# Sub-experts: half of the gates read from DRAM as repeated rows, and one product of four on GpSimd

## The chip, the cores and the metric

The kernel runs as one program on one core of a Trainium2 chip. The metric is device microseconds of one execution, lower is better. Before the change it takes 2109.84 us (median of three runs, 2108.4 to 2111.88).

## What is computed

The model is a chain of eight layers on 16 samples of 102 tokens with 192 features each. The change touches the sixth layer, a bank of small experts. Cut to what matters, with n over the 1632 tokens, s over 8 sets, m over 64 sub-experts of a set, r over 16 features, h over 32 hidden units:

```
z = einsum('nd,sdr->nsr', xf, P)
scores = einsum('nsr,smr->nsm', z, C)
topv, topi = top_k(scores, 4)
w = softmax(topv)
h = gelu(einsum('nsr,nskrh->nskh', z, W1[topi]) + b1[topi])
yl = einsum('nskh,nskhr->nskr', h, W2[topi]) + b2[topi]
comb = einsum('nskr,nsk->nsr', yl, w)
out = gelu(comb @ G1 + g1b) @ G2 + g2b
```

The kernel gathers nothing: it computes the hidden values of all 512 sub-experts for all tokens and multiplies each by its gate, which is zero for a sub-expert that was not chosen.

## The kernel before, in words

Two functions matter. `fusion_and_gates` (tiles named `l2b_...`) ends layer 5 and makes z and the gates. Per sample it transposes the gates of all 512 sub-experts into one PSUM bank as `[128, 4, 102]` (row = 64 * odd + m, four blocks r), copies them to `gT` in f32, and splits them into three bf16 parts whose sum is the f32 value: part 0 by a ScalarE copy (L1447), the rest by a VectorE subtraction (L1606), part 1 by another ScalarE copy (L1456), part 2 by GpSimd (L1159). SyncE stores the parts to the DRAM tensor `g_parts` after every four samples.

`sub_experts` (tiles `l2s_...`) is the stage of this case. Its work is 256 pairs, in the hand-written list `order`: (half of the samples, r, odd, t, pair). A pair is 128 hidden units (4 sub-experts of 32) for 8 samples, done as two chunks of 408 columns. For each pair:

- TensorE makes the hidden sums, two bf16 products of 128 x 408 (`up_products`, L2277).
- ScalarE applies bias and gelu to both chunks at once, 128 x 816 (L2352), into `hidden`.
- TensorE spreads the gates: the 4 gates of a chunk, each as three bf16 rows, are multiplied with a 0/1 matrix of 96 x 128, so that each gate stands on 32 partitions of a PSUM bank (`gates_spread`, L2285). Two per pair.
- VectorE multiplies hidden by gates, one chunk of 128 x 408 f32 at a time (L2382), into the ring `gated`.
- TensorE multiplies `gated` with the f32 down weights, four chunks at a time in four column groups (`second`, L2297); the sums of 32 such calls gather in one PSUM bank, and VectorE then adds them to `comb` (L2367, L2369).

Two pairs (four chunks) are called a group below; there are 128 groups. TensorE's order is written out in a loop: `up_products(p + 1)`, two spreads, and after every second pair a `second` of the group before. The gate banks are three, the `hidden` buffers three, the `gated` ring has ten chunks. All transfers of the stage are issued by SyncE (six by ScalarE) at its start, in program order, without a wait: z parts, up weights, gate parts, down weights for k = 0 to 3, then z and gate parts of the second half, then `pack_l3a` for the next layer. After the 128 groups comes a short tail: hidden products and results of four quarters.

Two transfers elsewhere in the program are used below for comparison. Layer 4 stores the tensor `up_pairs` (L772) in eight transfers of 512 KB; each goes from 128 partitions, written to DRAM as 8 sets x 16 rows x 2048 bf16 values. Layer 8 stores `xln` (L2488, L2489) from 102 partitions, written as 102 tokens x 16 samples x 192 (or 64) values.

Of the kernel before, what the change touches and what calls it, by code (L numbers as in the profile page):

```python
# [1023 lines left out]
def fusion_and_gates(nc, g, dram):  # L1024
# [8 lines left out]
    with ExitStack() as stack:  # L1033
# [13 lines left out]
        g_left = spare["l0a"].take(128, 4, L)  # L1047
# [14 lines left out]
        gT = m.sb("gT", [128, 4, GB, L])  # L1062
        g_parts = m.sb("g_parts", [128, 2, 3, 4, GB, L], BF16)
# [45 lines left out]
        gT_view = gT_bank.rearrange("p (r n) -> p r n", r=4)  # L1109

# [9 lines left out]
        def _(sp):  # L1120
            for c in range(G):
# [41 lines left out]
        def _(pe):  # L1163
# [91 lines left out]
            def bias_products(c, half):  # L1255
# [4 lines left out]
                for r in range(2):  # L1260
                    row = 64 * (c % 2) + HP * r
                    last = pe.matmul(gT_bank[row:row + HP], wf.at("b2", RG)[:, 2 * half + r, :], gT[:, 2 * half + r, :, :],
                                     start=True, stop=True)
# [91 lines left out]
        def _(act):  # L1355
# [49 lines left out]
            def step(t):  # L1405
# [37 lines left out]
                if 0 <= n < B:  # L1443
                    act.wait_ge(gT_ps, n + 1)
                    if n >= 2 * GB and n % GB == 0:
                        act.wait_ge(g_stored[n // GB % 2], 48 * (n // GB // 2))
# [34 lines left out]
        def _(dve):  # L1481
# [89 lines left out]
            def step(t):  # L1571
# [29 lines left out]
                if 0 <= e < B:  # L1601
# [4 lines left out]
                    dve.tensor_tensor(g_left[:, :, :], gT_view, g_parts[:, e // GB % 2, 0, :, e % GB, :], ALU.subtract)\  # L1606
# [566 lines left out]
def sub_experts(nc, g, dram):  # L2173
# [9 lines left out]
    pairs, per_sum_bank = len(order), len(order) // 2  # L2183
    with ExitStack() as stack:  # L2184
# [4 lines left out]
        gs = [[m.sb(f"gs{half}{k}", [96, 2, 2, HALF, L], BF16) for k in range(4)] for half in range(2)]  # L2189
# [7 lines left out]
        hid_ready, gated_ready = m.sem("hid_ready"), m.sem("gated_ready")  # L2197
# [12 lines left out]
        def gate_bank(n):  # L2210
            return ps[:, 1, n % gates, 0:NG]
# [9 lines left out]
        def gate_parts(eng, half, k):  # L2221
            for a in range(3):
                for n in range(2):
                    rows = 64 * (k % 2) + 32 * n
                    eng.dma_start(gs[half][k][32 * a:32 * (a + 1), n, :, :, :],
                                  g["g_parts"][a, rows:rows + 32, 2 * (k // 2):2 * (k // 2) + 2,
                                               half * HALF:(half + 1) * HALF, :]).then_inc(parts_loaded[half][k], 16)

        @block.sync
        def _(sp):  # L2230
# [17 lines left out]

            sp.dma_start(spread_raw, dram["sub_spread"]).then_inc(spread_loaded, 16)
            for half in range(2):  # L2250
                for k in range(4):
                    parts(half, k)
                    if not half:
                        up_weights(k)
                    if half or k:
                        gate_parts(sp, half, k)
                    if not half:
                        down_weights(k)
                    if not half and k == 2:
                        sp.dma_start(comb[:, :, :, :, :], g["sub_bias"]).then_inc(sums_loaded, 16)  # L2260
                        sp.dma_start(per_sum[:, :, :, :, :], g["sub_per_sum"]).then_inc(sums_loaded, 16)
# [4 lines left out]
        def _(pe):  # L2266
# [14 lines left out]
            def gates_spread(n):  # L2281
                half, r, odd, t, pair = order[n // 2]
                if n >= gates:
                    pe.wait_ge(gated_ready, n - gates + 1)
                pe.matmul(gate_bank(n), spread[:, t % 8, :], gs[half][2 * r + odd][:, t // 8, pair, chunk(n % 2), :],  # L2285
                          start=True, stop=True).then_inc(gate_ps, 1)

            def second(n):
                if n % per_sum_bank == 0 and n:
                    pe.wait_ge(comb_ready, n // per_sum_bank)  # L2290
                pe.wait_ge(gated_ready, n + group)
                for at in range(n, n + group):
                    half, r, odd, t, pair = order[at // 2]
                    if not half and t == 0 and pair == 0 and at % 2 == 0:
                        pe.wait_ge(down_loaded[2 * r + odd], 16)
                    row = HP * (2 * (at % 2) + pair)
                    last = pe.matmul(sums[row:row + HP, :], down[2 * r + odd][:, pair, t, :], gated[:, at % ring, :],  # L2297
                                     start=(odd == 0 and t == 0), stop=(odd == 1 and t == MT - 1))
                if (n + group) % per_sum_bank == 0:
# [748 lines left out]
```

## Time and profile before

| what | value |
|---|---|
| median of three runs | 2109.84 us |
| span of the profiled execution | 2092.6 us |
| what lies around the span, taken as the rest of the median | 17.2 us |
| `sub_experts`: first up product to last `second` | 1308.7 to 1631.5 us |
| busy over the whole span: PE, DVE, ACT, POOL | 1823.8, 1217.6, 837.4, 379.2 us |

The profile gives no run time of its own for the profiled execution beside its span; the runs shown agree within 0.2%. Times of rows are microseconds from the span's start. PE is TensorE's matmul, PEld its weight load, DVE VectorE, ACT ScalarE, POOL GpSimd, SPq SyncE issuing transfers. PEclk is the granted clock of TensorE (1.00 is 2.4 GHz, 0.50 is 1.2 GHz), DMA share the mean busy share of the core's 16 DMA engines, GB/s what they moved.

### The profile page before, as it was taken

How to read it: one execution, taken by the hardware profiler on the slowest of the kernel's cores; microseconds unless marked ns; L12 is line 12 of the kernel's file. 1: busy time of each engine (PE TensorE's matmuls, PEld its weight loads, DVE VectorE, ACT ScalarE, POOL GpSimd, SP SyncE). 2: the span in 40 equal slices, each digit the busy share in tenths (PEclk: the TensorE clock that was granted, in tenths of full speed). 3: DMA queues.
4: the chain of work that ended last, by engine and by line, in shares of the span. 5: the costliest groups of instructions: out<-in, count | busy, mean ns of one | idle time of the engine just before them, and what ended most of it. 6: DMA issues, size and time to landing. Idle time of an engine off the chain costs nothing. (4 is left out here: it accounts for less than half of the span.)

```text
span 2092.6 us, 38743 instructions
## 1 busy us (share of the span) xinstructions
PE 1823.8 (87%) x13908; PEld 1324.8 (63%) x14000; DVE 1217.6 (58%) x3641; ACT 837.4 (40%) x1667; POOL 379.2 (18%) x380
## 2 busy tenths in 40 slices
PE   4989969987886799888898875999999999979997
PEld 3678759966674699677665542333333688647886
DVE  1478842237998322378635554788888567891221
ACT  1145413324552111145435554677667355311111
POOL 1100112133312232331001111000000000223543
PEclk8999969998996899889999877999999999999999
DMA  5000245520003455102000115900000000304663
GB/s 202 1 1 0 108 131 178 187 74 18 14 0 141 142 186 182 38 19 87 0 1 17 38 49 145 292 2 1 1 1 1 24 1 0 134 22 124 197 173 65
DMA packets 83838, 156.75 MB, mean 75 GB/s; under 512 B 22389, under 2 KB 57941, under 8 KB 82805
## 3 DMA queue, kind: packets, MB, share of 16 engines
q1 hardware_dynamic: 63669, 134.71, 19.7%
q0 software_dynamic: 19552, 19.63, 3.9%
q8 instruction: 80, 1.31, 0.3%
q10 hardware_dynamic: 480, 0.63, 0.1%
q14 instruction: 57, 0.47, 0.1%
HBM read 125.04 MB, written 29.48 MB: 74 GB/s over the span
## 5 line engine op out<-in xcount | busy, mean ns | idle before, releaser
L2382 DVE TENSOR_TENSOR l2s_gated<-l2s_hidden,ps 128x408 f32<-128x408 f32 x512 | 262.8, 574 | 58.3 <-PE ps L2285 58.0
L2352 ACT ACTIVATE l2s_hidden<-ps,pack_l2f 128x816 f32<-128x816 f32 x256 | 227.2, 938 | 98.1 <-PE ps L2277 97.4
L129 PE MATMUL ps<-pack_const 128*128 128x512 bf16 x496 | 149.7, 437 | 42.2 <-PEq L163 15.3
L2285 PE MATMUL ps<-l2s_gs,l2s_spread 96*128 96x408 bf16 x512 | 150.8, 341 | 0.3 <-DVE l2s_gated L2382 0.3
L2277 PE MATMUL ps<-l2s_zs,l2s_up 128*128 128x408 bf16 x512 | 133.0, 342 | 14.5 <-DMA l2s_gs<-g_parts 14.5
L1895 PE MATMUL ps<-l_down,l_hidden 128*128 x792 | 139.8, 326 | 0.0
L1895 PEld LDWEIGHTS ps<-l_down,l_hidden 128*128 128x128 f32 x792 | 127.3, 190 | 0.4
L129 PEld LDWEIGHTS ps<-pack_const 128*128 128x128 bf16 x588 | 59.7, 109 | 102.1 <-issue 64.6
L2297 PE MATMUL ps<-l2s_gated,l2s_down 128*32 128x408 f32 x1024 | 114.3, 518 | 4.0 <-DVE l2s_comb L2369 3.7
L2277 PEld LDWEIGHTS ps<-l2s_zs,l2s_up 128*128 128x128 bf16 x512 | 39.8, 97 | 119.5 <-ACT l2s_hidden L2352 82.2
L1854 POOL DMA_INDIRECT l_xt<-rows_in,l_tokens x66 | 63.1, 956 | 255.7 <-PE ps L1867 196.5
L1878 PE MATMUL ps<-l_xtT,l_up 128*128 128x128 f32 x792 | 101.2, 278 | 3.4 <-DVE l_xtT L2145 3.4
L1878 PEld LDWEIGHTS ps<-l_xtT,l_up 128*128 128x128 f32 x792 | 98.3, 194 | 4.4 <-DVE l_xtT L2145 4.4
L2285 PEld LDWEIGHTS ps<-l2s_gs,l2s_spread 96*128 96x128 bf16 x512 | 50.1, 98 | 79.1 <-DVE l2s_gated L2382 49.5
L1974 ACT ACTIVATE l_hidden<-ps,l_down 128x128 f32<-128x128 f32 x198 | 54.8, 375 | 89.9 <-PE ps L1883 89.9
L2823 DVE TENSOR_TENSOR l3c_expert_hidden<-l3c_expert_gate,ps 128x204 f32<-128x204 f32 x96 | 30.9, 364 | 98.0 <-ACT l3c_expert_gate L2651 98.0
L1977 ACT ACTIVATE l_hidden<-ps 128x384 f32<-128x384 f32 x66 | 28.8, 488 | 143.2 <-PE ps L1883 143.2
L2651 ACT ACTIVATE l3c_expert_gate<-ps 128x204 f32<-128x204 f32 x96 | 27.4, 338 | 145.1 <-PE ps L2587 145.1
L2694 POOL DMA_INDIRECT out<-l3c_part,l3c_chosen_place x32 | 57.4, 1793 | 98.9 <-DVE l3c_part L2813 90.3
L2145 DVE TENSOR_SCALAR l_xtT<-ps,pack_l1r 128x128 f32<-128x128 f32 x66 | 24.0, 406 | 81.2 <-PE ps L1867 81.2
L2145 DVE TENSOR_SCALAR l_xtT<-ps,pack_l0r 128x128 f32<-128x128 f32 x66 | 24.1, 407 | 78.1 <-PE ps L1867 78.1
L496 POOL MEMSET l3a_v<- 102x408 f32 x2 | 1.0, 518 | 358.6 <-POOLq L2184 358.6
(468 smaller groups left out, 3985.0 us busy)
## 6 DMA issues: line engine op xcount, KB each, us to landing
l_up<-in_l_up SPq DMA_DIRECT2D x66, 576.0 KB, 3.8
l3c_wg<-in_l_gate SPq DMA_DIRECT2D x16, 576.0 KB, 4.9
l3c_wu<-in_l_up SPq DMA_DIRECT2D x16, 576.0 KB, 6.2
l3c_wd<-in_l_down SPq DMA_DIRECT2D x16, 576.0 KB, 3.9
slots_out<-l_y SPq DMA_DIRECT2D x66, 96.0 KB, 2.3
l_down<-in_l_down SPq DMA_DIRECT2D x8, 675.0 KB, 9.2
g_parts<-l2b_g_parts SPq DMA_DIRECT2D x12, 408.0 KB, 4.4
l_down<-in_l_down SPq DMA_DIRECT2D x8, 576.0 KB, 7.3
```

Source lines behind the costliest of these rows:

```text
L129: pe.matmul(bank, halves[:, 0:128], halves[:, :], start=True, stop=True)
L1854: pool.indirect_dma_start(xt[:, i % 3, :], None, xs, bass.IndirectOffsetOnAxis(ap=tokens[:, i:i + 1], axis=0))\
L1878: pe.matmul(hid_bank(i, half)[:, t * 128:(t + 1) * 128], up[:, i % 3, n * 128:(n + 1) * 128], xtT[:, i % 2, 0, :], start=(t == 0), stop=Fa ...
L1895: last = pe.matmul(y_bank(i), hidden[:, i % 2, t, :], wd[:, t * D:(t + 1) * D], start=(t == 0), stop=(t == FM - 1))
L1974: last = act.activation(hidden[:, i % 2, n, :], hid_bank(i, half)[:, t * 128:(t + 1) * 128], func, bias=b1[:, n:n + 1])
L2145: last = dve.tensor_scalar(xtT[:, i % 2, c, :], turned(i)[:, c * 128:(c + 1) * 128], w.at("wide_g")[:, c:c + 1], w.at("wide_b")[:, c:c + 1 ...
L2277: last = pe.matmul(ps[:, 0, 2 * (p % 2) + c, 0:NG], up_parts[k][:, pair, t * 128:(t + 1) * 128], zs[half][k][:, pair, chunk(c), :], start= ...
L2285: pe.matmul(gate_bank(n), spread[:, t % 8, :], gs[half][2 * r + odd][:, t // 8, pair, chunk(n % 2), :], start=True, stop=True).then_inc(ga ...
L2297: last = pe.matmul(sums[row:row + HP, :], down[2 * r + odd][:, pair, t, :], gated[:, at % ring, :], start=(odd == 0 and t == 0), stop=(odd ...
L2352: act.activation(hidden[:, p % kept, :, :], ps[:, 0, 2 * (p % 2):2 * (p % 2) + 2, 0:NG], ACT.Gelu_apprx_tanh, bias=w.at("b1")[:, s * MT + ...
L2382: dve.tensor_tensor(gated[:, n % ring, :], hidden[:, n // 2 % kept, n % 2, :], gate_bank(n), ALU.mult)\
L2694: pool.indirect_dma_start(table, bass.IndirectOffsetOnAxis(ap=chosen_place[:, a, e:e + 1], axis=0), part[:, e % 2, a, :], None, compute_op ...
```

## The change

Half of the gates, those of the pairs with pair = 1, are no longer spread by TensorE. `fusion_and_gates` keeps the bf16 parts of blocks 0 and 2 only, and stores blocks 1 and 3 in f32 to a new DRAM tensor `g_whole`. `sub_experts` reads them back with one transfer per group: four rows of 816 values (3264 bytes), each repeated 32 times, into one of six buffers `whole` of 128 x 816. The first six are issued between the up weights and the down weights of k = 0, the others behind all transfers of the first half, each waiting until its buffer is free. Of a group's four chunks VectorE multiplies two with gates in PSUM (L2417) and one with gates in `whole` (L2424), and GpSimd the fourth with gates in `whole` (L2395). `hidden` gets four buffers, `gated` shrinks to eight chunks, and `second` now comes after the next up products.

```diff
-        g_left = spare["l0a"].take(128, 4, L)
+        g_left = spare["l0a"].take(128, 2, L)
...
-        gT = m.sb("gT", [128, 4, GB, L])
-        g_parts = m.sb("g_parts", [128, 2, 3, 4, GB, L], BF16)
+        gT = m.sb("gT", [128, 2, 4, GB, L])
+        g_parts = m.sb("g_parts", [128, 2, 3, 2, GB, L], BF16)
...
+        gT_split = gT_view[:, 0:4:2, :]
...
+                sp.dma_start(g["g_whole"][:, :, there, :], gT[:, c % 2, 1:4:2, :, :]).then_inc(g_stored[c % 2], 16)
...
-                    act.activation(g_parts[:, n // GB % 2, 0, :, n % GB, :], gT_view, ACT.Copy)
-                    if n >= GB and n % GB == 0:
-                        act.wait_ge(b2_ps, 2 * (n // GB))
-                    act.activation(gT[:, :, n % GB, :], gT_view, ACT.Copy).then_inc(gT_ready, 1)
+                    act.activation(g_parts[:, n // GB % 2, 0, :, n % GB, :], gT_split, ACT.Copy)
+                    if n >= 2 * GB and n % GB == 0:
+                        act.wait_ge(b2_ps, 2 * (n // GB - 1))
+                    act.activation(gT[:, n // GB % 2, :, n % GB, :], gT_view, ACT.Copy).then_inc(gT_ready, 1)
...
-                    dve.tensor_tensor(g_left[:, :, :], gT_view, g_parts[:, e // GB % 2, 0, :, e % GB, :], ALU.subtract)\
+                    dve.tensor_tensor(g_left[:, :, :], gT_split, g_parts[:, e // GB % 2, 0, :, e % GB, :], ALU.subtract)\
...
-    gates, kept, group, ring = 3, 3, 4, 10
+    gates, kept, group, ring, ahead = 3, 4, 4, 8, 6
...
+        whole = m.sb("whole", [128, ahead, 2, NG])
...
+            def whole_gates(n):
+                half, r, odd, t, _ = order[2 * n]
+                row = 64 * odd + 4 * t
+                if n >= ahead:
+                    sp.wait_ge(gated_ready, 3 * (n - ahead + 1))
+                    sp.wait_ge(late_ready, n - ahead + 1)
+                sp.dma_start(whole[:, n % ahead, :, :].rearrange("p c n -> p (c n)"),
+                             g["g_whole"][row:row + 4, r, half * HALF:(half + 1) * HALF, :]
+                             .rearrange("e b l -> e (b l)").unsqueeze(1).broadcast_to([4, 32, HALF * L]))\
+                  .then_inc(whole_loaded[n % ahead], 16)
...
-            for half in range(2):
-                for k in range(4):
-                    parts(half, k)
-                    if not half:
-                        up_weights(k)
-                    if half or k:
-                        gate_parts(sp, half, k)
-                    if not half:
-                        down_weights(k)
...
+            for k in range(4):
+                parts(0, k)
+                up_weights(k)
+                if k:
+                    gate_parts(sp, 0, k)
+                else:
+                    for n in range(ahead):
+                        whole_gates(n)
+                down_weights(k)
...
+            for n in range(ahead, groups):
+                if n % 8 == 0 and 2 <= n // 8 < 6:
+                    parts(1, n // 8 - 2)
+                    gate_parts(sp, 1, n // 8 - 2)
+                whole_gates(n)
             sp.dma_start(g["pack_l3a"][:, :], dram["pack_l3a"]).then_inc(pack_loaded, 16)
...
+                pe.wait_ge(gated_ready, 3 * (n + 1))
+                pe.wait_ge(late_ready, n + 1)
...
-                for n in (2 * p, 2 * p + 1):
-                    gates_spread(n)
-                if p >= 3 and p % 2 == 1:
-                    second(2 * p - 6)
-            second(2 * pairs - group)
+                if p % 2 == 0:
+                    gates_spread(p // 2)
+                elif p >= 3:
+                    second(p // 2 - 1)
+            second(groups - 1)
...
+        @block.gpsimd
+        def _(pool):
+            for n in range(groups):
+                pool.wait_ge(gate_ps, 2 * n + 1)
+                pool.wait_ge(whole_loaded[n % ahead], 16 * (n // ahead + 1))
+                pool.wait_ge(hid_ready, 2 * n + 2)
+                pool.tensor_tensor(gated[:, (4 * n + 3) % ring, :], hidden[:, (2 * n + 1) % kept, 1, :],
+                                   whole[:, n % ahead, 1, :], ALU.mult).then_inc(late_ready, 1)
...
-                dve.tensor_tensor(gated[:, n % ring, :], hidden[:, n // 2 % kept, n % 2, :], gate_bank(n), ALU.mult)\
-                   .then_inc(gated_ready, 1)
+            for n in range(groups):
+                dve.wait_ge(hid_ready, 2 * n + 1)
+                for c in range(2):
+                    dve.wait_ge(gate_ps, 2 * n + c + 1)
+                    dve.tensor_tensor(gated[:, (4 * n + c) % ring, :], hidden[:, 2 * n % kept, c, :], gate_bank(2 * n + c),
+                                      ALU.mult).then_inc(gated_ready, 1)
...
+                dve.wait_ge(whole_loaded[n % ahead], 16 * (n // ahead + 1))
+                dve.wait_ge(hid_ready, 2 * n + 2)
+                dve.tensor_tensor(gated[:, (4 * n + 2) % ring, :], hidden[:, (2 * n + 1) % kept, 0, :],
+                                  whole[:, n % ahead, 0, :], ALU.mult).then_inc(gated_ready, 1)
```

TensorE inside the stage, one group, before (L2277 up products, L2285 spreads, L2297 `second`):

```order
L2277 MATMUL ps<-l2s_zs,l2s_up 128x408 x2
L2285 MATMUL ps<-l2s_gs,l2s_spread 128x408 x2
L2277 MATMUL ps<-l2s_zs,l2s_up 128x408 x2
L2285 MATMUL ps<-l2s_gs,l2s_spread 128x408 x2
L2297 MATMUL ps<-l2s_gated,l2s_down 32x408 x4
```

and with the change (L2298 up products, L2308 spreads, L2322 `second`):

```order
L2298 MATMUL ps<-l2s_zs,l2s_up 128x408 x2
L2308 MATMUL ps<-l2s_gs,l2s_spread 128x408 x2
L2298 MATMUL ps<-l2s_zs,l2s_up 128x408 x2
L2322 MATMUL ps<-l2s_gated,l2s_down 32x408 x4
```

Two of the four spreads of a group are gone.

SyncE's transfers at the start of the stage, before:

```order
L2249 DMA l2s_gated<-in_sub_spread 96x1024
L2245 DMA l2s_zs<-z_pairs 128x2x816
L2233 DMA l2s_up<-up_pairs 128x2x2048
L2238 DMA l2s_down<-in_sub_down 128x2x512
L2245 DMA l2s_zs<-z_pairs 128x2x816
L2233 DMA l2s_up<-up_pairs 128x2x2048
L2225 DMA l2s_gs<-g_parts 32x2x816 x6
```

and with the change:

```order
L2250 DMA l2s_zs<-z_pairs 128x2x816
L2238 DMA l2s_up<-up_pairs 128x2x2048
L2260 DMA l2s_whole<-g_whole 128x1x816 x6
L2243 DMA l2s_down<-in_sub_down 128x2x512
L2250 DMA l2s_zs<-z_pairs 128x2x816
L2238 DMA l2s_up<-up_pairs 128x2x2048
L2230 DMA l2s_gs<-g_parts 32x816 x6
```

Six `whole` transfers stand ahead of the first down weights; a seventh comes behind the down weights of k = 3.

## Rows read from the trace of the kernel before

**Rows 1.** Windows of the stage (columns as its first row names them)
```profile
core 0: us, PE busy (x) PEld busy (x) DVE busy (x) ACT busy (x) POOL busy (x), PEclk, DMA share, GB/s
1310.00:1631.00 321.00, 316.63 (x2041) 109.42 (x2043) 265.79 (x518) 226.70 (x256) 0.00 (x0) 0.99 0.16 46
1400.00:1450.00 50.00, 50.00 (x328) 17.05 (x320) 41.63 (x82) 36.00 (x41) 0.00 (x0) 1.00 0.00 1
```
**Rows 2.** Timeline, one group: start, us, engine, line, operation, [idle before <-releaser]
```profile
1452.48 0.52 PE L2277 MATMUL ps<-l2s_zs,l2s_up 128*128 128x408 bf16 x2
1453.03 1.77 ACT L2352 ACTIVATE l2s_hidden<-ps,pack_l2f 128x816 f32<-128x816 f32 x2 [0.69 <-PE ps L2277]
1453.20 2.05 DVE L2382 TENSOR_TENSOR l2s_gated<-l2s_hidden,ps 128x408 f32<-128x408 f32 x4 [0.42 <-PE ps L2285]
1454.12 0.89 PE L2297 MATMUL ps<-l2s_gated,l2s_down 128*32 128x408 f32 x8
1454.94 0.52 PE L2277 MATMUL ps<-l2s_zs,l2s_up 128*128 128x408 bf16 x2
```
**Rows 3.** SyncE's timeline and windows around the stores of `up_pairs`
```profile
958.40 7.69 SPq L772 DMA_DIRECT2D up_pairs<-pack_l1a  x5
968.94 1.24 SPq L772 DMA_DIRECT2D up_pairs<-pack_l0a  x1
...
974.00:976.00 2.00, 2.00 (x32) 1.72 (x34) 1.43 (x8) 1.80 (x4) 0.70 (x1) 1.00 0.52 211
978.00:980.00 2.00, 2.00 (x14) 2.00 (x13) 1.86 (x5) 1.18 (x2) 0.00 (x0) 1.00 0.51 209
```
**Rows 4.** The same two views around the stores of `xln`
```profile
1805.54 0.29 SPq L2488 DMA_DIRECT2D xln<-l3c_x  x1
...
1812.00:1813.00 1.00, 1.00 (x4) 0.56 (x3) 0.96 (x2) 0.00 (x0) 0.00 (x0) 1.00 0.41 139
```
**Rows 5.** Windows in the stage's loading phase
```profile
1298.00:1358.40 60.40, 49.73 (x304) 17.75 (x305) 43.02 (x81) 37.51 (x42) 0.00 (x0) 0.86 1.05 297
1300.00:1305.00 5.00, 0.00 (x0) 0.00 (x0) 2.19 (x3) 2.34 (x2) 0.00 (x0) 0.50 1.04 288
1326.00:1327.00 1.00, 1.00 (x9) 0.31 (x7) 0.93 (x2) 1.00 (x2) 0.00 (x0) 1.00 1.00 418
1335.00:1336.00 1.00, 1.00 (x9) 0.49 (x6) 0.58 (x3) 0.30 (x2) 0.00 (x0) 1.00 1.04 222
```
**Rows 6.** Transfers issued from 1295 to 1365 us: count, KB each, median us to landing
```profile
l2s_gs<-g_parts SPq DMA_DIRECT2D x42, 102.0 KB, 11.6
...
pack_l3a<-in_pack_l3a SPq DMA_DIRECT2D x1, 1299.0 KB, 15.1
```
**Rows 7.** Timeline at the stage's start and end
```profile
1308.67 1.52 PE L2277 MATMUL ps<-l2s_zs,l2s_up 128*128 128x408 bf16 x4 [14.47 <-DMA l2s_gs<-g_parts]
...
1324.74 1.21 SPq L2238 DMA_DIRECT2D l2s_down<-in_sub_down  x1
...
1630.64 0.89 PE L2297 MATMUL ps<-l2s_gated,l2s_down 128*32 128x408 f32 x8 [0.30 <-DVE l2s_gated L2382]
```
**Rows 8.** Products with both inputs in SBUF: ns min/median/max, first and last start
```profile
L2668 POOL TENSOR_TENSOR l3c_hidden<-l3c_act_gate,l3c_act_up x12: 1042/1043/1054, 1814.0 to 1864.7; 128x408 f32<-128x408 f32 x12
L2369 DVE TENSOR_TENSOR l2s_comb<-l2s_comb,l2s_per_sum x4: 582/582/585, 1394.3 to 1632.2; 128x408 f32<-128x408 f32 x4
```
**Rows 9.** Timeline where a VectorE and a GpSimd instruction overlap
```profile
1202.91 0.94 POOL L1159 TENSOR_TENSOR l2b_g_parts<-pack_l0a,l2b_g_parts 128x408 bf16<-128x408 f32 x1 [0.64 <-ACT l2b_g_parts L1456]
1202.97 1.69 DVE L1524 TENSOR_TENSOR rows_z<-rows_z,o_all 102x768 f32<-102x768 f32 x1
1204.58 0.95 DVE L1527 TENSOR_TENSOR h<-h,pack_l2a 102x768 f32<-102x768 f32 x1
```
**Rows 10.** ScalarE's timeline in `fusion_and_gates`, one step
```profile
1266.32 0.49 ACT L1447 ACTIVATE l2b_g_parts<-ps 128x408 bf16<-128x408 f32 x1
...
1267.85 0.54 ACT L1456 ACTIVATE l2b_g_parts<-pack_l0a 128x408 bf16<-128x408 f32 x1 [0.47 <-DVE pack_l0a L1606]
```

More of the change, by code:

```diff
@@ L1261, in bias_products @@
                     row = 64 * (c % 2) + HP * r
-                    last = pe.matmul(gT_bank[row:row + HP], wf.at("b2", RG)[:, 2 * half + r, :], gT[:, 2 * half + r, :, :],
+                    last = pe.matmul(gT_bank[row:row + HP], wf.at("b2", RG)[:, 2 * half + r, :], gT[:, c % 2, 2 * half + r, :, :],
                                      start=True, stop=True)
@@ L2183, in sub_experts @@
     pairs, per_sum_bank = len(order), len(order) // 2
+    groups, in_bank = pairs // 2, pairs // 8
     with ExitStack() as stack:
@@ L2188, in sub_experts @@
         zs = [[m.sb(f"zs{half}{k}", [128, 2, HALF, L], BF16) for k in range(4)] for half in range(2)]
-        gs = [[m.sb(f"gs{half}{k}", [96, 2, 2, HALF, L], BF16) for k in range(4)] for half in range(2)]
+        gs = [[m.sb(f"gs{half}{k}", [96, 2, HALF, L], BF16) for k in range(4)] for half in range(2)]
+        whole = m.sb("whole", [128, ahead, 2, NG])
         comb = m.sb("comb", [128, 2, 2, GB, L])
@@ L2196, in sub_experts @@
         up_ps, gate_ps = m.sem("up_ps"), m.sem("gate_ps")
-        hid_ready, gated_ready = m.sem("hid_ready"), m.sem("gated_ready")
+        hid_ready, gated_ready, late_ready = m.sem("hid_ready"), m.sem("gated_ready"), m.sem("late_ready")
+        whole_loaded = [m.sem(f"whole_loaded{k}") for k in range(ahead)]
         comb_ps, comb_ready, comb_added = m.sem("comb_ps"), m.sem("comb_ready"), m.sem("comb_added")
@@ L2224, in gate_parts @@
                     rows = 64 * (k % 2) + 32 * n
-                    eng.dma_start(gs[half][k][32 * a:32 * (a + 1), n, :, :, :],
-                                  g["g_parts"][a, rows:rows + 32, 2 * (k // 2):2 * (k // 2) + 2,
-                                               half * HALF:(half + 1) * HALF, :]).then_inc(parts_loaded[half][k], 16)
+                    eng.dma_start(gs[half][k][32 * a:32 * (a + 1), n, :, :],
+                                  g["g_parts"][a, rows:rows + 32, k // 2, half * HALF:(half + 1) * HALF, :])\
+                       .then_inc(parts_loaded[half][k], 16)
         @block.sync
@@ L2281, in gates_spread @@
             def gates_spread(n):
[L2282 to L2286, printed above, removed]
-            def second(n):
[L2289 to L2299, printed above, removed]
+                half, r, odd, t, _ = order[2 * n]
@@ new lines, in gates_spread @@
+                for c in range(2):
+                    j = 2 * n + c
+                    if j >= gates:
+                        pe.wait_ge(gated_ready, 3 * ((j - gates) // 2) + (j - gates) % 2 + 1)
+                    pe.matmul(gate_bank(j), spread[:, t % 8, :], gs[half][2 * r + odd][:, t // 8, chunk(c), :],
+                              start=True, stop=True).then_inc(gate_ps, 1)
+            def second(n):
+                half, r, odd, t, _ = order[2 * n]
+                if n % in_bank == 0 and n:
+                    pe.wait_ge(comb_ready, n // in_bank)
+                pe.wait_ge(gated_ready, 3 * (n + 1))
+                pe.wait_ge(late_ready, n + 1)
+                if not half and t == 0:
+                    pe.wait_ge(down_loaded[2 * r + odd], 16)
+                for pair in range(2):
+                    for c in range(2):
+                        row = HP * (2 * c + pair)
+                        last = pe.matmul(sums[row:row + HP, :], down[2 * r + odd][:, pair, t, :],
+                                         gated[:, (4 * n + 2 * pair + c) % ring, :],
+                                         start=(odd == 0 and t == 0), stop=(odd == 1 and t == MT - 1))
+                if (n + 1) % in_bank == 0:
```

29 lines of the change are left out of this document (15 added, 14 removed).

## The prediction

> **What bounds the kernel now.** I read the windows of the stage first. From 1310 to 1631 us TensorE is busy 316.6 of 321 us at clock 0.99, VectorE 265.8, ScalarE 226.7, GpSimd nothing, and after the loading phase the DMA share is 0.00 [rows 1]. So TensorE bounds the stage, and the transfer engines and GpSimd are free: the change moves work onto exactly these two. The timeline of one group shows the pace: the up products start at 1452.48 and again at 1454.94, so a group lasts 2.46 us [rows 2], and 128 of them 315 us. In it TensorE needs 0.82 us for `second` (1454.12 to 1454.94) and about 0.17 us for each bf16 product (0.52 us for two, of which one is latency of a single one, 0.35). VectorE has 2.05 us of work for four products and waits 0.42; ScalarE has 1.77 and waits 0.69 [rows 2].
>
> **The new transfer decides, so it comes first.** Every group now needs 128 rows of 3264 bytes, 417,792 bytes; 128 groups make 53.5 MB. On all 16 DMA engines that would be easy: 418 GB/s at share 1.00 for the big rows, 222 GB/s at share 1.04 for the rows of 1632 bytes [rows 5], hence 1.0 to 1.9 us a group. But the source is written as 4 rows x 32 repeats x 816, and its slowest dimension is 4. What a small slowest dimension does stands elsewhere in this trace. The eight stores of `up_pairs` have 128 partitions on the SBUF side, but 8 sets as the slowest dimension in DRAM. SyncE had issued the last by 970.2 us, a backlog was waiting, and still the DMA share stood at 0.51 to 0.52 until 980, with 209 to 211 GB/s [rows 3]: half of the engines moved nothing, the other eight moved 26.1 to 26.4 GB/s each. The store of `xln`, with 102 rows slowest on both sides, runs at share 0.41 for microseconds [rows 4]; 6 is the largest number up to 16 that divides 102, and 6/16 is 0.375. So I read: a transfer is dealt out over its slowest dimension to the largest number of engines up to 16 that divides it on both sides. With 4 against 128 that is **four engines of sixteen**.
>
> The Trainium skill says the same in "DMA: Bandwidth & Descriptors", section "Why a DMA increments its semaphore by 16 and not by 1": the engine count is the largest one up to 16 that divides the slowest non-unit dimension of both access patterns, and on a SyncE queue the lowest-numbered engines are taken. By that rule too, every one of the 128 loads would lie on the same four engines; the trace agrees with the rule in the shares 0.51 and 0.41, but has no load with a slowest dimension of 4, nor does it tell which engines carry a transfer.
>
> Price of one load on four engines, from both sides. Floor: 418/16 = 26.1 GB/s per engine, four make 104.5 GB/s, 4.0 us. Far end: the 1632-byte rows give 222/16 = 13.9 GB/s per engine, so 7.5 us. By the time per row, 117 ns for 1632 bytes at 13.9 GB/s and 157 ns for 4096 bytes at 26.1 GB/s make 144 ns for 3264 bytes between them, times 32 rows per engine, 4.6 us. The slow rows were read while all sixteen engines loaded DRAM; here twelve are idle, so I take a value between floor and interpolation, **4.3 us**. For the upper end of the range I take the mixed rate at the start of the stage, 288 GB/s at share 1.04 [rows 5], four engines of which give 72 to 75 GB/s, 5.6 us.
>
> **The stage, step by step.** A load of 4.3 us is longer than the whole present group of 2.46 us, so the six buffers ahead only fill once and the stage runs at the pace of its four loaded engines. Their work, one thing after the other:
> - The loading phase as before kept all engines busy from 1298 to 1358.4 us, 60.4 us at share 1.05 [rows 5]. Of it goes half of the gate parts: 48 transfers of 102 KB [rows 6] (42 of SyncE and 6 of ScalarE) are 5.0 MB, half of that at 222 GB/s is 11.3 us. `pack_l3a`, 1299 KB, comes after the last `whole` load now and goes from this sum with 3.5 us; it lands beside the tail of the stage. Rest: 45.6 us.
> - 128 loads x 4.3 us = 550.4 us (4.0 us: 513; 5.6 us: 717).
> - The last load lands at 1298 + 45.6 + 550.4 = 1894.0 us. Then come a VectorE product of 0.58 us [rows 8] and the last `second` with 0.89 us; end 1895.6. Before, it ended at 1630.64 + 0.89 = 1631.5 [rows 7]. Difference **+264 us**.
>
> Compute is covered by this. TensorE loses two spreads of 0.17 us a group and would need about 6 x 0.17 + 0.82 + 0.1 = 1.95 us. With the waits it will hardly keep its clock: at 1.2 GHz (clock 0.50 stood at the stage's start, where four products took 1.52 us, 0.34 each beyond the first [rows 7]) a group is 6 x 0.34 + 1.64 = 3.7 us, still under 4.3. GpSimd's product costs 1.04 us and VectorE's with two SBUF inputs 0.58 [rows 8]; SyncE's issue of one load, about 0.5 us, fits. The lower clock does reach into the tail of the stage, where TensorE is not covered: +3 us, by guess of a few products at half speed.
>
> In `fusion_and_gates` the parts shrink from 408 to 204 columns: two ScalarE copies (0.49 and 0.54 us) and the VectorE subtraction between them, for which ScalarE waits 0.47 us [rows 10]. By the length alone each would lose about 0.2 us, 0.6 us a step, 16 steps 10 us if all lay on the path; ScalarE also waits for other things in a step, so I take -6 us (0 to -10). The four extra stores of 408 KB lie between others of SyncE and before the bias, which is not waited for: nothing.
>
> Sum: +264 - 6 + 3 = +261. The span of 2092.6 us becomes 2354; with the 17.2 us that lie around it, 2371 us, which is the median 2109.84 plus the same 261.
>
> **Rivals.**
> 1. *All sixteen engines carry the loads* (the repeated source is split otherwise than the stores were, or the larger side decides). Against it: both stores above. For it: neither was a load, and neither repeated a row. Then loads of 1.0 to 1.9 us hide, and the stage is bound by a chain over two groups: up product 0.35 + 0.2 to ScalarE, gelu 0.94, GpSimd 1.04, VectorE's SBUF product 0.58, `second` 0.9, hand-overs 0.2, in all 4.2, or 2.1 us a group. GpSimd and VectorE count one after the other there: VectorE's L1524, with two SBUF inputs, took 1.69 us beside a GpSimd subtraction and ended 0.81 us after it, where its like took 0.95 alone [rows 9]. 128 x (2.46 - 2.1) = 46 us gained. Lost again at the start: the seventh load stands behind 13.8 MB, at some 320 GB/s until 1341 us, where group 6 would want it at about 1327: 14 us. Result 2110 - 46 + 14 - 6 = **2072 us**. In this rival the two products might also not collide: the group is then 1.95 us, and the result 2053.
> The Trainium skill has the collision in "SBUF — State Buffer", section "Who interferes with whom": a VectorE instruction with two SBUF inputs and a GpSimd instruction that reads SBUF exclude each other for a whole instruction. [rows 9] agree in one place; the rule is worth 19 us, 2072 against 2053, and only in this rival.
> 2. *The loads are much slower than 5.6 us*, because four engines read one row of DRAM 32 times over. For it: 1632-byte rows at 13.9 GB/s per engine. 7.5 us a load gives 1298 + 45.6 + 960 = 2304, +672: **2779 us**.
> 3. *The change gains and loses nothing*: loads of about 2.1 us, on eight engines. The result would be near rival 1, up to 2.46 us a group. Nothing in the rows gives eight for a dimension of 4.
>
> **How the numbers follow.** Four engines at 4.0 to 5.6 us: 0.82. Rival 2 and all beyond 5.6 us: 0.08. Rivals 1 and 3: 0.09 faster, 0.01 the same. That makes slower by over 0.2% 0.90, within 0.2% (4 us, about what a measurement of this kernel can tell) 0.01, faster 0.09. The predicted time is that of the forecast, 2371. Range: with 4.0 us a load 2334, and as the rest of the loading might run faster with less beside it, 2325; with 5.6 us 2537. 2325 to 2537 us holds the forecast's 0.82.
>
> **What would show it.** Right: over the stage a DMA share near 0.25 and about 97 GB/s instead of 0.00; VectorE and GpSimd waiting for the DMA of `whole` in most groups; landing of a load some 26 us after its issue (six in flight); TensorE below half busy, clock 0.50 in long stretches; the stage about 585 us long. At its start the down weights of k = 0, behind six loads on the same engines, arrive around 1330 us. Wrong: a DMA share near 0.5 or more in the stage (rival 1), groups of 2 us with waits between VectorE and GpSimd; or a share of 0.25 at only 55 GB/s (rival 2).

## The result and the profile after

The changed kernel takes 2344.21 us (median of four runs, 2338.51 to 2350.08) beside 2109.12 us for the kernel before, a ratio of 1.1109 with a 95% interval of 1.1085 to 1.1134. The profiled execution is the slowest of the four, 2350.08 us, and spans 2348.3 us. The head of its page, three of the costliest groups and one row of the issues:

```profile
span 2348.3 us, 38479 instructions
PE 1840.5 (78%) x13652; PEld 1320.8 (56%) x13744; DVE 1157.3 (49%) x3513; ACT 837.3 (36%) x1667; POOL 551.6 (23%) x508
...
L2322 PE MATMUL ps<-l2s_gated,l2s_down 128*32 128x408 f32 x1024 | 135.9, 604 | 239.3 <-DVE l2s_gated L2417 199.5
L2395 POOL TENSOR_TENSOR l2s_gated<-l2s_hidden,l2s_whole 128x408 f32<-128x408 f32 x128 | 176.2, 1377 | 410.4 <-ACT l2s_hidden L2380 215.8
L2424 DVE TENSOR_TENSOR l2s_gated<-l2s_hidden,l2s_whole 128x408 f32<-128x408 f32 x128 | 77.1, 603 | 327.5 <-DMA l2s_whole<-g_whole 308.4
...
l2s_whole<-g_whole SPq DMA_DIRECT2D x128, 408.0 KB
```

VectorE's new product (L2424) runs 77.1 us in all, and VectorE sat idle 308.4 us before it until the load of `whole` was there. That is more than the whole loss of 235 us. The windows of the stage, in the columns of [rows 1]:

```profile
1330.00:1340.00 10.00, 0.00 (x0) 0.00 (x0) 0.00 (x0) 0.00 (x0) 0.00 (x0) 0.50 0.73 189
1600.00:1700.00 100.00, 61.70 (x350) 18.99 (x342) 39.78 (x77) 45.31 (x50) 34.24 (x25) 0.85 0.26 104
1700.00:1800.00 100.00, 61.40 (x348) 19.03 (x349) 39.56 (x76) 43.74 (x49) 33.91 (x26) 0.84 0.26 104
```

Against 316.6 busy us of 321 and a DMA share of 0.00 [rows 1], TensorE is now busy 61%, 25 groups pass in 100 us, and the share stands at 0.26 with 104 GB/s. I read this as a quarter of the transfer engines working all the time and the others not at all; the share alone doesn't tell that, the experiments below do. The timeline of a group shows who waits (start, duration; in brackets the idle time before and what ended it):

```profile
1648.06 0.93 PE L2322 MATMUL ps<-l2s_gated,l2s_down 128*32 128x408 f32 x4
1648.93 0.86 PE L2298 MATMUL ps<-l2s_zs,l2s_up 128*128 128x408 bf16 x2
...
1649.72 0.58 DVE L2424 TENSOR_TENSOR l2s_gated<-l2s_hidden,l2s_whole 128x408 f32<-128x408 f32 x1 [2.39 <-DMA l2s_whole<-g_whole]
1649.82 1.39 POOL L2395 TENSOR_TENSOR l2s_gated<-l2s_hidden,l2s_whole 128x408 f32<-128x408 f32 x1 [2.56 <-issue]
...
1650.24 1.07 DVE L2417 TENSOR_TENSOR l2s_gated<-l2s_hidden,ps 128x408 f32<-128x408 f32 x2
...
1651.36 0.89 PE L2322 MATMUL ps<-l2s_gated,l2s_down 128*32 128x408 f32 x8 [0.21 <-DVE l2s_gated L2417]
1652.19 0.52 PE L2298 MATMUL ps<-l2s_zs,l2s_up 128*128 128x408 bf16 x2
...
1653.68 0.58 DVE L2424 TENSOR_TENSOR l2s_gated<-l2s_hidden,l2s_whole 128x408 f32<-128x408 f32 x1 [2.37 <-ACT l2s_hidden L2380]
```

L2424 starts at 1649.72 and again at 1653.68: 3.96 us a group, where it was 2.46 [rows 2]. GpSimd's product is stretched to 1.39 us beside VectorE's. The two up products at 1648.93 take 0.86 us, those at 1652.19, in the next group, 0.52 us.

Where the time went, from the stage's first SyncE transfer to the end of the last `second`: before, 1297.1 to 1631.5, 334.4 us; after, 1309.1 to 1885.2, 576.1 us: **+241.7**. `fusion_and_gates`, from its first product on `l2b_lin_f` to SyncE's last store of `sub_per_sum`, takes 7.5 us less (rows in experiment 9). What follows the stage lasts 463.1 us against 461.1: +2. Together +236.2, against +235.1 between the medians. (Run 9, a second profile of the kernel before, gives the same stage, 334.3 us, and the same rest, 461.0. Its span is 239.9 us shorter than that of the changed kernel; the 3.5 us that are missing lie ahead of `fusion_and_gates`, in code that the change leaves alone.)

### The profile page after: what moved, and what is told of

Read it like the earlier page. It is cut to its first block and busy times, and to the rows that moved or that the text cites. A ratio compares the mean times of both kernels' runs of the same rounds, so it can differ in the third digit from the quotient of the medians.

```text
span 2348.3 us, 38479 instructions
## 1 busy us (share of the span) xinstructions
PE 1840.5 (78%) x13652; PEld 1320.8 (56%) x13744; DVE 1157.3 (49%) x3513; ACT 837.3 (36%) x1667; POOL 551.6 (23%) x508
## 5 line engine op out<-in xcount | busy, mean ns | idle before, releaser
L2380 ACT ACTIVATE l2s_hidden<-ps,pack_l2f 128x816 f32<-128x816 f32 x256 | 232.5, 939 | 328.8 <-PE ps L2298 327.3
L2322 PE MATMUL ps<-l2s_gated,l2s_down 128*32 128x408 f32 x1024 | 135.9, 604 | 239.3 <-DVE l2s_gated L2417 199.5
L2395 POOL TENSOR_TENSOR l2s_gated<-l2s_hidden,l2s_whole 128x408 f32<-128x408 f32 x128 | 176.2, 1377 | 410.4 <-ACT l2s_hidden L2380 215.8
L2424 DVE TENSOR_TENSOR l2s_gated<-l2s_hidden,l2s_whole 128x408 f32<-128x408 f32 x128 | 77.1, 603 | 327.5 <-DMA l2s_whole<-g_whole 308.4
L2322 PEld LDWEIGHTS ps<-l2s_gated,l2s_down 128*32 128x32 f32 x1024 | 25.2, 117 | 303.7 <-DVE l2s_gated L2417 259.1
L2298 PE MATMUL ps<-l2s_zs,l2s_up 128*128 128x408 bf16 x512 | 162.9, 408 | 12.1 <-DMA l2s_up<-up_pairs 12.1
L2417 DVE TENSOR_TENSOR l2s_gated<-l2s_hidden,ps 128x408 f32<-128x408 f32 x256 | 136.0, 573 | 30.7 <-PE ps L2308 30.6
L2298 PEld LDWEIGHTS ps<-l2s_zs,l2s_up 128*128 128x128 bf16 x512 | 45.2, 109 | 147.1 <-issue 100.8
L2308 PE MATMUL ps<-l2s_gs,l2s_spread 96*128 96x408 bf16 x256 | 83.3, 414 | 0.0
L546 PE MATMUL ps<-l2a_xT,pack_l2a 96*128 96x204 f32 x240 | 58.2, 404 | 12.5 <-ACT xT_all L673 12.5
```

The lines of the kernel that those rows point to most:

```text
L2298: last = pe.matmul(ps[:, 0, 2 * (p % 2) + c, 0:NG], up_parts[k][:, pair, t * 128:(t + 1) * 128], zs[half][k][:, pair, chunk(c), :], start= ...
L2308: pe.matmul(gate_bank(j), spread[:, t % 8, :], gs[half][2 * r + odd][:, t // 8, chunk(c), :], start=True, stop=True).then_inc(gate_ps, 1)
L2380: act.activation(hidden[:, p % kept, :, :], ps[:, 0, 2 * (p % 2):2 * (p % 2) + 2, 0:NG], ACT.Gelu_apprx_tanh, bias=w.at("b1")[:, s * MT + ...
L2395: pool.tensor_tensor(gated[:, (4 * n + 3) % ring, :], hidden[:, (2 * n + 1) % kept, 1, :], whole[:, n % ahead, 1, :], ALU.mult).then_inc(l ...
L2417: dve.tensor_tensor(gated[:, (4 * n + c) % ring, :], hidden[:, 2 * n % kept, c, :], gate_bank(2 * n + c), ALU.mult).then_inc(gated_ready, 1)
L2424: dve.tensor_tensor(gated[:, (4 * n + 2) % ring, :], hidden[:, (2 * n + 1) % kept, 0, :], whole[:, n % ahead, 0, :], ALU.mult).then_inc(ga ...
```

## The experiments

Times are compared by the ratio to the kernel before on the same chip. Diffs are against the changed kernel.

**1. The repeat as slowest dimension (rep32).** The same rows are read 32 times each, but the repeats are outermost; hidden unit j of sub-expert e then stands on partition 4j + e, so up weights, bias, down weights and the 0/1 matrix are permuted on the host (`units`).

```diff
-                             .rearrange("e b l -> e (b l)").unsqueeze(1).broadcast_to([4, 32, HALF * L]))\
+                             .rearrange("e b l -> e (b l)").unsqueeze(1).unsqueeze(0)
+                             .broadcast_to([REPEAT, 4, 32 // REPEAT, HALF * L]))\
```

> The changed kernel, with the repeats as the slowest dimension of the source: 32 repeats x 4 rows x 816 instead of 4 x 32 x 816. The hidden units of four sub-experts are laid out to match (unit-major), in up weights, b1, down weights and the 0/1 matrix. Same bytes, same rows of 3264 bytes, each still read 32 times. Theory A (a transfer goes to the largest number of engines up to 16 that divides the slowest dimension of both sides; 4 before, 16 here): a load takes 1.0 to 1.9 us of all engines and hides, the stage is bound by compute at 2.1 us a group plus a stall at its start, about 2072 us. Rival B (reading one row of DRAM 32 times is what is slow, whatever the engines): about 2344 us, as the changed kernel. Rival C (the stage is held by the products on VectorE and GpSimd, not by the loads): 2344 us too.

Measured: 2065.15 us, ratio 0.9795 (0.9773 to 0.9818). One window of the stage, its groups, and a piece of the timeline:

```profile
1400.00:1500.00 100.00, 95.14 (x655) 30.98 (x655) 96.17 (x146) 82.81 (x94) 49.01 (x47) 0.98 0.64 205
```

```profile
L2426 DVE TENSOR_TENSOR l2s_gated<-l2s_hidden,l2s_whole 128x408 f32<-128x408 f32 x128 | 143.4, 1121 | 12.2 <-DMA l2s_whole<-g_whole 12.2
L2397 POOL TENSOR_TENSOR l2s_gated<-l2s_hidden,l2s_whole 128x408 f32<-128x408 f32 x128 | 134.9, 1054 | 176.4 <-ACT l2s_hidden L2382 162.7
```

```profile
1406.71 1.05 POOL L2397 TENSOR_TENSOR l2s_gated<-l2s_hidden,l2s_whole 128x408 f32<-128x408 f32 x1 [0.92 <-ACT l2s_hidden L2382]
...
1407.13 1.07 DVE L2426 TENSOR_TENSOR l2s_gated<-l2s_hidden,l2s_whole 128x408 f32<-128x408 f32 x1
...
1408.77 1.05 POOL L2397 TENSOR_TENSOR l2s_gated<-l2s_hidden,l2s_whole 128x408 f32<-128x408 f32 x1 [1.01 <-ACT l2s_hidden L2382]
```

The loss is gone, with the same bytes and the same 32 reads of each row: share 0.64 and 205 GB/s in place of 0.26 and 104. So neither the volume nor the repeated reading cost the time, but the dimension that stood outermost. The groups come every 2.04 us, and VectorE, busy 96.17 of 100 us, now sets the pace: its SBUF product takes 1.12 us and not 0.58 [rows 8] beside GpSimd's.

**2, 3. Eight and two rows in the slowest dimension (rows8, rows2).** The bytes and the partitions stay; the gates land on wrong sub-experts. The diff is that of rows8, without the line that keeps the last rows inside the tensor; rows2 has 2 and 64 in place of 8 and 16.

```diff
-                             g["g_whole"][row:row + 4, r, half * HALF:(half + 1) * HALF, :]
-                             .rearrange("e b l -> e (b l)").unsqueeze(1).broadcast_to([4, 32, HALF * L]))\
+                             g["g_whole"][row:row + 8, r, half * HALF:(half + 1) * HALF, :]
+                             .rearrange("e b l -> e (b l)").unsqueeze(1).broadcast_to([8, 16, HALF * L]))\
```

> The changed kernel, but a load reads 8 neighbouring rows 16 times each instead of 4 rows 32 times (gates land on wrong sub-experts; bytes and row length as before). Theory A: eight engines, 209 GB/s, 2.0 us a load. The 16-engine loads of the stage's start come on top, so the stage lasts about 12 + 46 + 128 x 2.0 = 314 us where 576 us were measured: about 2080 us. Rival B (repeated reads of a row): half as many reads of each row, between 2080 and 2344 us, with a DMA share above 0.5 if engines queue at the row. Rival C: 2344 us.

> The changed kernel, but a load reads 2 neighbouring rows 64 times each (gates land on wrong sub-experts; bytes and row length as before). Theory A: two engines, DMA share 0.125 and 52 GB/s over the stage, 8.0 us a load, 512 us more than the changed kernel: about 2856 us. Rival C: 2344 us.

Measured: 2096.73 and 2854.61 us (one run each). A window in the stage of eight rows, then one at the start of the stage of two rows:

```profile
1500.00:1550.00 50.00, 48.40 (x340) 16.02 (x344) 48.78 (x73) 41.82 (x49) 24.68 (x24) 1.00 0.52 205
```

```profile
1320.00:1340.00 20.00, 0.00 (x0) 0.00 (x0) 2.15 (x4) 0.00 (x0) 2.76 (x2) 0.52 0.13 52
```

Two, four and eight rows give shares of 0.13, 0.26 and 0.52 with 52, 104 and 205 GB/s, which fits two, four and eight engines of sixteen at about 26 GB/s each. (For two rows 0.13 and 52 GB/s stand again in the window from 1700 to 1800 us.) The Trainium skill, "DMA: Bandwidth & Descriptors", section "Why a DMA increments its semaphore by 16 and not by 1", has the rule for the number of engines: the largest one up to 16 that divides the slowest dimension of both sides. The three shares agree with it. For two rows the time came out as expected within 2 us. For eight it is 17 us above. At 2.0 us a load just keeps pace with a group, and where other transfers run beside it, it doesn't: VectorE waits 29.8 us for `whole` over the stage (12.2 us in rep32), 11.1 of them between 1400 and 1500 us, and TensorE 13.5 us for the down weights.

**4. No loads after the first six groups (noload).**

```diff
-                whole_gates(n)
...
-                pool.wait_ge(whole_loaded[n % ahead], 16 * (n // ahead + 1))
+                pool.wait_ge(whole_loaded[n % ahead], 16)
```

> The changed kernel without the loads of groups 6 to 127: the six buffers keep their first contents (old gates are used), no group waits for a load after the sixth. What is left is compute. Theory: 2.1 us a group, because GpSimd's product and VectorE's product with two SBUF inputs exclude each other; the stage from its first transfer to the last second product 15 + 25 (six loads on four engines ahead of the down weights) + 269 = 309 us, about 2344 - 576 + 309 = 2077 us. Rival (they do not hold each other up): 1.95 us a group, about 2058 us. Rival C (compute is what lasts 4.2 us a group): 2344 us.

Measured: 2076.1 us (one run). The groups take 2.02 us (2.04 in rep32) with a DMA share of 0.00 later in the stage, so the transfers of rep32 cost next to nothing there. But at the start TensorE waits 26.6 us for the down weights, which stand behind the six loads; SyncE's six issues alone last 17.1 us:

```profile
L2423 DVE TENSOR_TENSOR l2s_gated<-l2s_hidden,l2s_whole 128x408 f32<-128x408 f32 x128 | 142.1, 1110 | 3.6 <-DMA l2s_whole<-g_whole 3.6
...
L2321 PE MATMUL ps<-l2s_gated,l2s_down 128*32 128x408 f32 x1024 | 117.7, 532 | 35.7 <-DMA l2s_down<-in_sub_down 26.6 <-DVE l2s_comb L2405 6.3 <-DVE l2s_gated L2423 1.9
```

VectorE's product is 1.11 us here too, without any transfer beside it, so the stretch doesn't come from the transfers. Run 6 shows that it comes from GpSimd.

**5. The load cut in four (four).** The original order of hidden units, but one transfer for each row of gates. (VectorE and GpSimd then wait for 64 counts where they waited for 16, not shown.)

```diff
+                for e in range(4):
+                    sp.dma_start(whole[32 * e:32 * (e + 1), n % ahead, :, :].rearrange("p c n -> p (c n)"),
+                                 g["g_whole"][row + e:row + e + 1, r, half * HALF:(half + 1) * HALF, :]
+                                 .rearrange("e b l -> e (b l)").broadcast_to([32, HALF * L]))\
+                      .then_inc(whole_loaded[n % ahead], 16)
```

> Edit: the changed kernel with its original order of hidden units, but the load of a group is cut in four transfers, each of one row of gates (816 numbers) repeated to 32 partitions; nothing is left out of the computation. The slowest dimension of each transfer is now the repeat (32), where it was the row (4). If the four-row dimension is what confines a load to four DMA engines, each part is spread over all sixteen, and the share while they run is above 0.4. What is then open is the price of four issues on SyncE in place of one: if one takes about 0.45 us, 1.8 us a group hide under the group's 2.04 us and the time is that of the run with the repeat outermost, 2065 us; if it takes 0.65 us or more, 2.6 us a group bound the stage and it is 2065 + 128 x 0.56 = 2137 us (2126 to 2140). If the confinement were by bytes or by the number of rows read and not by the dimension, a group would still take 4.0 us and the time would stay at 2344 us.

Measured: 2060.53 us, ratio 0.9835 (0.9794 to 0.9876); this chip ran the kernel before in 2090.69 us. A window of the stage, then the rows of the new product and of SyncE's issues (ns min/median/max):

```profile
1400.00:1500.00 100.00, 95.59 (x663) 31.42 (x660) 95.90 (x144) 83.08 (x94) 49.06 (x47) 0.99 0.74 211
```

```profile
L2425 DVE TENSOR_TENSOR l2s_gated<-l2s_hidden,l2s_whole 128x408 f32<-128x408 f32 x128 | 142.2, 1111 | 15.8 <-DMA l2s_whole<-g_whole 15.5
```

```profile
L2261 SPq DMA_DIRECT2D l2s_whole<-g_whole x41: 302/421/1237, 1440.0 to 1459.6; - x41
```

The share is 0.74 where it was 0.26, and four issues of 0.42 us hide under a group. The layout of before can stay, and the interval of the ratio overlaps that of rep32 (in us it is 30 below its own chip's kernel before, rep32 44). Every transfer still reads its one row 32 times, so the cause of the loss is settled: neither the repeats nor the few rows, but that four of them stood outermost.

**6. VectorE does all four products (dve4, on rep32).**

```diff
+                dve.tensor_tensor(gated[:, (4 * n + 3) % ring, :], hidden[:, (2 * n + 1) % kept, 1, :],
+                                  whole[:, n % ahead, 1, :], ALU.mult).then_inc(late_ready, 1)
```

> As rep32 (repeats slowest in the source, loads on sixteen engines), but VectorE multiplies all four chunks and GpSimd none. Theory: in rep32 VectorE's product with two SBUF inputs takes 1.08 to 1.15 us beside GpSimd's 1.05 instead of 0.58, so GpSimd's help is spent on the wait; VectorE's four products have a pitch of 0.51 to 0.52 us, 2.07 us a group against 2.04 in rep32: within 10 us of rep32's 2065 us, at 2065 to 2075. Rival (GpSimd's product is a real quarter off VectorE): 0.5 us a group more, 65 us, 2130 us.

Measured: 2059.57 us, ratio 0.9758 (0.9734 to 0.9783).

```profile
L2422 DVE TENSOR_TENSOR l2s_gated<-l2s_hidden,l2s_whole 128x408 f32<-128x408 f32 x128 | 73.9, 577 | 12.4 <-DMA l2s_whole<-g_whole 12.2
L2424 DVE TENSOR_TENSOR l2s_gated<-l2s_hidden,l2s_whole 128x408 f32<-128x408 f32 x128 | 73.8, 577 | 0.0
```

I had expected a small loss against rep32, and it is no slower; it may be some us faster. GpSimd's product took 0.58 us off VectorE and gave 0.54 back as a stretch (1.12 less 0.58). As the change places it, GpSimd's help is worth nothing.

**7. SyncE's loads in another order (order, on rep32).** The down weights of k = 0 go behind the second `whole` load instead of the sixth, and the sets k = 2 and 3, the bias and the second half are spread between the groups.

```diff
-            for k in range(4):
...
+            first_half(0)
+            for n in range(2, ahead):
+                whole_gates(n)
+            first_half(1)
+            for n in range(ahead, groups):
+                if n in (12, 22):
+                    first_half(2 + (n == 22))
```

> As rep32, with SyncE's loads in another order: down weights of k = 0 behind the second load of gates, the loads of k = 2 and 3, of the bias sums and of the second half set between later loads of gates, so that the seventh load of gates no longer stands behind 13.8 MB. Theory: the stall of the first groups (in rep32 VectorE waits 12.2 us for a load and GpSimd 13.7) goes: 12 us less than rep32, about 2053 us. Rival: another load is late in its place (up or down weights of k = 1), and no more than 4 us are gained.

Measured: 2054.31 us, ratio 0.9719 (0.9692 to 0.9747), about as expected. VectorE's wait for `whole` goes from 12.2 to 2.9 us, and TensorE's for the down weights, 2.5 us in rep32, is gone:

```profile
L2433 DVE TENSOR_TENSOR l2s_gated<-l2s_hidden,l2s_whole 128x408 f32<-128x408 f32 x128 | 143.3, 1120 | 2.9 <-DMA l2s_whole<-g_whole 2.9
...
L2331 PE MATMUL ps<-l2s_gated,l2s_down 128*32 128x408 f32 x1024 | 117.4, 531 | 13.4 <-DVE l2s_comb L2415 6.2 <-DVE l2s_gated L2426 3.8 <-DVE l2s_gated L2433 2.0
```

**8. GpSimd beside the PSUM products (late6, on order).** GpSimd starts when VectorE's SBUF product is done, so that it runs beside the two products that read PSUM; `second` comes a group later, and the ring `gated` has 12 places.

```diff
-                pool.wait_ge(gate_ps, 2 * n + 1)
...
+                pool.wait_ge(gated_ready, 3 * (n + 1))
```

> As order, and GpSimd's product of a group waits for VectorE's product with two SBUF inputs of the same group, so that it runs beside VectorE's two products with PSUM inputs of the next group; the second product comes one group later, the ring of gated values holds twelve chunks. Theory (the two instructions exclude each other, and only those): VectorE needs 1.05 + 0.52 = 1.57 us a group and TensorE bounds at 1.95 to 1.97; 0.07 us x 128 = 9 us less than order, about 2044 us, VectorE's SBUF product back at 0.58 us. Rival (GpSimd slows VectorE's PSUM products as well): VectorE's products take longer throughout, and the time is that of order or more.

Measured: 2038.81 us (2035.57 to 2042.71), ratio 0.9662 (0.9636 to 0.9687), faster than both kernels, the best of the study and 5 us below what I had expected.

```profile
1440.00:1500.00 60.00, 59.76 (x428) 19.90 (x429) 48.79 (x93) 53.66 (x61) 32.34 (x31) 1.00 0.72 220
```

```profile
L2427 DVE TENSOR_TENSOR l2s_gated<-l2s_hidden,ps 128x408 f32<-128x408 f32 x256 | 136.7, 575 | 45.8 <-PE ps L2317 45.5
L2405 POOL TENSOR_TENSOR l2s_gated<-l2s_hidden,l2s_whole 128x408 f32<-128x408 f32 x128 | 135.5, 1059 | 144.0 <-DVE l2s_gated L2434 142.4
L2434 DVE TENSOR_TENSOR l2s_gated<-l2s_hidden,l2s_whole 128x408 f32<-128x408 f32 x128 | 76.9, 601 | 5.8 <-DMA l2s_whole<-g_whole 5.8
```

The SBUF product is back at 0.60 us on average (0.577 in the median), the PSUM products stay at 0.575 us though GpSimd runs beside them, and TensorE is busy 59.76 of 60 us: it bounds the stage again, with two spreads a group fewer.

**9. The kernel before once more (before_again), unchanged.**

> The kernel before, profiled once more. Layer 5 (860 to 1060 us), whose code the change leaves alone, lasted 12 to 19 us longer in all five profiles of changed kernels, at a lower granted clock. If that is chance or a drift of the chip, this profile shows it too: first product on l2b_lin_f near 1058 us. If it belongs to the changed kernels, this one has it at 1046 us, as the first profile.

Measured: 2110.12 us, span 2108.4. The first fence is this run, the second the changed kernel: the first products on `l2b_lin_f` and SyncE's last store of `sub_per_sum`.

```profile
L1189 PE MATMUL ps<-l2b_lin_f x64: 251/253/333, 1062.1 to 1182.9; 96*102 96x102 f32 x64
...
1309.79 0.49 SPq L1137 DMA_DIRECT2D sub_per_sum<-l2b_per_sum  x1
```

```profile
L1191 PE MATMUL ps<-l2b_lin_f x64: 251/253/334, 1065.6 to 1185.7; 96*102 96x102 f32 x64
...
1305.85 0.49 SPq L1139 DMA_DIRECT2D sub_per_sum<-l2b_per_sum  x1
```

From the one to the other 247.7 us pass before and 240.2 after: −7.5 for `fusion_and_gates`. The start itself, 1062.1, lies 16 us later than in the profile that I predicted from (1046.1), in the same kernel.

## Why the prediction was right

The forecast was 2371 us, the result is 2344, inside the range of 2325 to 2537 and on the side that had 0.90. That it came so near is in part luck: two terms of the stage were wrong in opposite directions, by −38 and +16 us.

- **Four engines of sixteen.** Right, and shown: share 0.26 where it said 0.25; two and eight rows scale as two and eight engines (runs 2, 3); repeats outermost, or one row a transfer, lift the share to 0.64 and 0.74 (runs 1, 5), more than eight engines can give. It was read from two stores with 8 and 102 rows, [rows 3] and [rows 4], and holds for a load with a repeated source.
- **4.3 us a load.** The mis-sized term: 100 us hold 25 groups, 4.0 us each, which was the floor. I lifted it because the rows are shorter than 4096 bytes, going by the slow rows of 1632; 104 GB/s on four engines is the full 26 GB/s per engine of the big rows [rows 5]. 128 x 0.3 = 38 us too much. (The far end of the range, 5.6 us, needs 75 GB/s; the windows it was read from give 72 and 74, so 5.6 to 5.8. It wasn't needed.)
- **45.6 us for the rest of the loading.** Too little; it was 61. The seventh product starts at 1379.1:

```profile
L2424 DVE TENSOR_TENSOR l2s_gated<-l2s_hidden,l2s_whole x21: 582/583/585, 1379.1 to 1466.6; 128x408 f32<-128x408 f32 x21
```

  That is 70 us after the first transfer, of which seven loads are 28, so 42 for other transfers; from there to the last, at 1882.0, 502.9 us pass for 121 loads of 4.0 = 484, another 19. I had let the rest run on all engines at share 1.05, but mixed with the loads it doesn't: 1330 to 1340 us stands at 0.73. Which transfers lie badly was not taken apart. Both errors together are −38 + 16 = −22, the stage's difference (+264 forecast, +241.7 measured).
- **The end of the stage.** As said, last load, product, `second`. The forecast counted from a stage that starts at 1297.1, and in the profile after it starts at 1309.1, so 1885.2 has to be set against 1895.6 + 12 = 1907.6: the same 22 us.
- **`fusion_and_gates` −6, tail +3.** −7.5 and +2. The +3 was called a guess, and the runs don't bear out its reason: from the end of the stage to the first product on `l3a_v` in the next layer 36.5 us pass after and 36.1 before, so whatever the stage's end cost its tail is 0.4 us at most. The rest of the +2 lies later and was not taken apart. Nor was the −7.5 taken apart by steps.
- **TensorE's clock.** Half wrong. "Below half busy, clock 0.50 in long stretches" was 61% busy at a granted clock of 0.77 (1400 to 1500 us) rising to 0.86. Both levels, 0.50 and 1.00, stand in the timeline: two up products in 0.86 us at 1648.93, and in 0.52 us at 1652.19. The clock doesn't follow the single waits: it fell at 1644.4 in the middle of a group's products, a wait of 2.0 us having ended at 1643.3; it came back at about 1651.3, after products without a pause from 1647.4 to 1651.2; and it stayed at 1.00 through the next two waits, of 1.9 and 2.9 us. So only a part of the groups had the 3.7 us of compute that I had counted for 1.2 GHz throughout. It changed nothing, since either lies under the load.
- **Down weights of k = 0 at about 1330.** They were late as said, behind the six loads, but later still: the first `second` starts at 1350.1, after 26.9 us of waiting. With the 12 us by which this stage starts later, the forecast stood for 1342. SyncE was held as well, which I had not counted:

```profile
1310.53 16.77 SPq L2260 DMA_DIRECT2D l2s_whole<-g_whole  x6
1327.34 4.01 SPq L2243 DMA_DIRECT2D l2s_down<-in_sub_down  x1
```

  The six issues took 2.8 us each, not the 0.5 that the forecast gave one, so the down weights were asked for only at 1327.
- **The other signs.** VectorE's new product waited for the load in 116 of 128 groups, as said; GpSimd's did in 28 and mostly waited for ScalarE's `hidden`. The landing of a load 26 us after its issue can't be tested: the profile gives no landing for these transfers.
- **Rival 1's numbers.** Its condition was false, but its sum can be tested in rep32: 2072 forecast, 2065 measured. The group was 2.04 us (2.1 forecast); the start lost 20 us (14 forecast: 128 x 0.42 = 54 gained, 33.6 left in the stage), of which run 7 took 11 back by the medians, 16 by the ratios. The collision of GpSimd and VectorE was real.
- **The 17.2 us around the span.** Not what it was called. Time and span differ by 1.7 us in run 9; the other 15.5 us are the 16 us by which `fusion_and_gates` starts earlier in the profile shown before than in that of run 9. It cancelled, since the sum was a difference.

## What to carry to other kernels

Ahead of using a transfer that repeats rows, read its slowest dimension on both sides: with two, four and eight rows outermost it ran on as many engines, at 26 GB/s each, and the DMA share of the stage tells it at once (0.26 for four). Put a large repeat (32 here) outermost, or issue one transfer for each row if the queue has the time. A GpSimd product beside a VectorE product with two SBUF inputs gained nothing here: start it beside a VectorE instruction that reads PSUM.

## What the runs showed of the hardware that I had not expected

- **Who is stretched.** In both places looked at, whichever of the two SBUF products starts second pays. In rep32 GpSimd starts at 1406.71 and ends at 1407.76; VectorE, started at 1407.13, ends 0.44 us after it, with 0.58 us of work. In the changed kernel VectorE starts 0.10 us ahead, takes its 0.58 us, and GpSimd needs 1.39 instead of 1.05. The Trainium skill, "SBUF — State Buffer", section "Who interferes with whom", says that whichever issues first takes the shared port for its whole instruction and the other blocks fully, and that VectorE with one SBUF input doesn't contend. By these numbers the second still finishes 0.14 us sooner than it would if it began only when the first ended, so the traces nearly agree; the PSUM products beside GpSimd took 0.575 us, unstretched, which agrees.
- **Reading one row 32 times costs nothing on four engines, and a little engine time where more carry it.** On four engines the loads ran at the rate of big distinct rows. In rep32 the rate is as the groups ask for it, 205 GB/s, and nothing waits for the loads in the steady part; but the share for it is 0.64, which makes about 20 GB/s for each engine's worth of busy time (205 / (16 x 0.64)), where four engines had 25 (104 / (16 x 0.26)). In late6 it is 19, in four 18. What makes the engines slower there, more of them at the same rows or fewer rows for each in a transfer, was not tried.
- **An issue is not always half a microsecond.** With loads of 4.0 us lined up, SyncE's issue of one took 3.78 us in the median of the changed kernel, 0.51 us in rep32. The first six, ahead of which the program has no wait, show that it is the issue and not a wait of the program (16.77 us above):

```profile
L2260 SPq DMA_DIRECT2D l2s_whole<-g_whole x128: 499/3776/8480, 1310.5 to 1857.3; - x128
```

- **A stage of unchanged code moves by up to 20 us between profiles.** The first product on `l2b_lin_f` starts at 1046.1, 1062.1, 1065.6, 1058.6 and 1048.7 us in before, before_again, after, rep32 and four, and one chip ran the kernel before in 2090.69 us where three other sets of runs had 2109 to 2112. In the profile of before, 920 to 1000 us stands at a granted clock of 1.00, in before_again, after and rep32 at 0.87 to 0.89. What decides this was not tried. A stage is therefore compared here from its own start to its own end, and not by its time in the profile.
